# Attention and routed experts on one core: the attention turn in another order, with v's sum and the expert pieces' low halves on VectorE

## The reference

```python
x = L0_attn_x
xn = _layernorm(x, axis=-1)
x = x + attention(xn, Wq, bq, Wk, bk, Wv, bv, Wo, bo, projection) + moe(xn, router_w, w1, w2)
```

## Time and profile before

| | |
|---|---|
| median of 3 runs | 1439.71 us (1437.99 to 1441.45) |
| the profiled execution | 1445.27 us |
| its span, first to last instruction | 1443.7 us |
| mean granted TensorE clock | 0.914 |
| TensorE busy in the span | 1250.0 us, 87% |
| VectorE | 819.6 us, 57% |
| ScalarE | 662.9 us, 46% |
| GpSimd | 763.1 us, 53% |

### The profile page before, as it was taken

The page is one execution under the profiler, slowest core; times in us unless marked ns, Lnnn a source line. Parts: engine busy times, 40 slices in busy tenths (PEclk is TensorE's granted clock), DMA queues, the critical chain, the costliest instruction groups (busy, mean ns, idle before and its releaser), DMA issues.

```text
span 1443.7 us, 38151 instructions
## 1 busy us (share of the span) xinstructions
PE 1250.0 (87%) x14334; PEld 994.5 (69%) x14334; DVE 819.6 (57%) x1910; ACT 662.9 (46%) x1140; POOL 763.1 (53%) x692
## 2 busy tenths in 40 slices
PE   4787777878787887754999999999999999999997
PEld 2555445455555554532878888888888888888886
DVE  6795867777786968682534444344444444344442
ACT  3776657677576766741323233332323333332322
POOL 3445445565455454673355555565555555565553
PEclk9888888888888878966999999999999999999999
DMA  4032333132323323325964444444444444344451
GB/s 156 28 107 89 118 88 119 30 129 76 107 75 89 118 75 118 119 72 171 279 167 73 80 75 73 71 75 78 75 75 76 79 75 78 68 78 74 78 78 15
DMA packets 156139, 133.73 MB, mean 93 GB/s; under 512 B 93825, under 2 KB 144258, under 8 KB 154946
## 3 DMA queue, kind: packets, MB, share of 16 engines
q1 hardware_dynamic: 122338, 95.58, 23.2%
q0 software_dynamic: 33632, 35.71, 15.6%
HBM read 61.83 MB, written 52.61 MB: 79 GB/s over the span
## 4 chain that ended last, share of the span: by engine, by line
PE 63%; DVE 16%; ACT 9%; DMA 5%; issue 4%; POOL 3%; SPq 0%; DVEq 0%; ACTq 0%; POOLq 0%
PE bank L948 26%; PE bank L964 25%; DMA area<-in_x_dram 3%; DVE area L1332 2%; DVE area L1218 2%; ACT area L512 2%; PE bank L825 2%; PE bank L732 2%; PE bank L811 2%; DVE area L1198 2%; PE bank L741 1%; ACT area L514 1%; ACT area L582 1%; ACT area L565 1%; ACT area L577 1%
## 5 line engine op out<-in xcount | busy, mean ns | idle before, releaser
L948 PE MATMUL bank<-area 128*128 128x256 f16 x3408 | 387.7, 274 | 18.7 <-DMA area<-xg 15.7
L964 PE MATMUL bank<-area 128*128 x3408 | 383.5, 273 | 0.0
L948 PEld LDWEIGHTS bank<-area 128*128 x3408 | 335.2, 98 | 60.1 <-issue 19.5
L1474 DVE TENSOR_SCALAR area<-area 128x512 f16<-128x512 f32 x284 | 128.5, 452 | 423.1 <-ACT area L639 414.3
L964 PEld LDWEIGHTS bank<-area 128*128 128x128 f16 x3408 | 333.3, 98 | 38.8
L1142 POOL DMA_INDIRECT out_dram<-area,mt x142 | 228.5, 1609 | 240.2 <-ACT area L649 213.7
L639 ACT ACTIVATE area<-bank 128x512 f32<-128x512 f32 x284 | 169.5, 597 | 190.0 <-PE bank L948 189.0
L649 ACT ACTIVATE area<-bank,mt 128x256 f32<-128x256 f32 x142 | 59.5, 470 | 329.5 <-PE bank L964 329.5
L1476 DVE SCALAR_TENSOR_TENSOR area<-area 128x512 f16<-128x512 f32 x284 | 196.7, 693 | 9.8
L1050 POOL DMA_INDIRECT slot_table<-area x128 | 136.7, 1068 | 121.3 <-DVE dump_f L1311 78.7
L1135 POOL DMA_INDIRECT xg<-xn_split,mt x142 | 143.5, 1010 | 44.7 <-issue 43.0
(11 more groups left out here) (178 smaller groups left out, 1499.1 us busy)
## 6 DMA issues: line engine op xcount, KB each, us to landing
area<-in_w_dram SPq DMA_DIRECT2D x32, 512.0 KB, 6.3
experts_split<-area SPq DMA_DIRECT2D x32, 512.0 KB, 4.3
area<-experts_split SPq DMA_DIRECT2D x8, 2048.0 KB, 8.0
area<-in_x_dram SPq DMA_DIRECT2D x16, 512.0 KB, 5.9
xn_split<-area SPq DMA_DIRECT2D x16, 512.0 KB, 3.0
out_dram<-area SPq DMA_DIRECT2D x32, 256.0 KB, 2.7
xg<-xn_split,mt POOLq DMA_INDIRECT x142, 2.9
area<-xg SPq DMA_TRANSPOSE x142
```

What stands on the lines that cost most here:

```text
L948: mm = nc.tensor.matmul(big[j][:, i2 * TS:(i2 + 1) * TS], we[:, bass.ds(e * EXPERT + (k * 2048 + wl * 1024 + c * P), P)], moe_xT[t % XT][: ...
L964: mm = nc.tensor.matmul(yb[:, a * D:(a + 1) * D], hT[u % 2][:, c, hl, a * P:(a + 1) * P], we[:, bass.ds(e * EXPERT + off, D)], start=(c == ...
L1474: v.tensor_scalar(hT[u % 2][:, 2 * j:2 * j + 2, 0, :], h32[j], H_SCALE, None, ALU.mult).then_inc(mh_step, 1)
```

## The change

- Key features of groups 0 and 1 (`k_features`, `k_relu`) of batch b + 1 are made at the end of turn b, not at the start of turn b + 1.
- Bank 7, the one of the key-value sums, also serves as a fourth small bank, for seven uses in a ring of its own with one place (`SIDE`); the other uses share the three banks as before.
- x has six half-batch buffers, and both halves of b + 2 are loaded at the start of the turn. The normalised x (`xn`) now has both halves and lies in the memory of the squares (`sq`). `grow` and `shift` are double.
- `v_total` is one reduction on VectorE. `w_low` moves from GpSimd to VectorE and takes the unscaled piece with the factor; ScalarE no longer scales the piece in place but in the rounding.
- The order of all five engines changes: both normalised halves before the key-value copy; the count of ranks after the query features; `o_transpose`, `square_sums`, `square_turn` and `o_project` at other places; `v_over_norm` of the second half at the end of the turn before; `tile_table` behind the key-value copy of the last turn; expert stores later.

```diff
-HALVES = 5
+HALVES = 6
...
-BODY = (attn("rank", "vsum", "kvT") + prep("xT0", "xT1") + attn("cn", "ab0", "ab1", "ab2", "ab3") + prep("xT2", "xT3")
-        + attn("ab4", "ab5", "ab6", "ab7") + prep("v0", "v1", "nrm0", "v2", "nrmT0", "v3") + attn("oT0", "oT1", "out0", "out1")
-        + attn("oT2", "oT3") + prep("v4", "v5") + attn("out2", "out3") + prep("v6", "nrm1", "v7", "nrmT1"))
+BODY = (attn("vsum", "kvT") + prep("xT0", "xT1") + attn("rank", "cn", "ab0", "ab1", "ab2", "ab3")
+        + prep("xT2", "xT3") + attn("ab4", "ab5", "ab6", "ab7") + prep("v0", "v1", "nrm0", "v2", "v3", "nrmT0") + attn("oT0", "oT1")
+        + attn("out0", "out1", "oT2", "oT3") + prep("nrm1", "v4", "v5", "nrmT1") + attn("out2", "out3")
+        + prep("v6", "v7"))
...
+SIDE = ("kvT", "cn", "nrm0", "nrmT0", "out0", "nrm1", "nrmT1")
...
+RINGS = {side: [u for u in SEQ if (u[1] in SIDE) == side] for side in (False, True)}
+SLOT = {use: n for ring in RINGS.values() for n, use in enumerate(ring)}
...
-    n = SLOT[(use[0], use[1], b)]
-    return n % SMALL_BANKS, SEQ[n - SMALL_BANKS] if n >= SMALL_BANKS else None
+    side = use[1] in SIDE
+    n, depth = SLOT[(use[0], use[1], b)], 1 if side else SMALL_BANKS
+    return SMALL_BANKS if side else n % SMALL_BANKS, RINGS[side][n - depth] if n >= depth else None
...
-        small = [bank[0], bank[1], bank[6]]
+        small = [bank[0], bank[1], bank[6], bank[7]]
...
-        xn = view([HT, D], F32)
...
+        xn = sq.rearrange("p a b c -> p (a b c)").rearrange("p (h t d) -> p h t d", h=2, t=HT)
...
             if body and x_next:
                 x_load(sp, b + 2, 0)
+                x_load(sp, b + 2, 1)
             if body:
                 xs_store(sp, b + 1, 0)
+                xs_store(sp, b + 1, 1)
             w_store(sp, b, 0)
             w_load(sp, b, 2)
-            if body:
-                xs_store(sp, b + 1, 1)
             w_store(sp, b, 1)
             w_load(sp, b, 3)
-            w_store(sp, b, 2)
-            if body:
-                w_load(sp, b + 1, 0)
             out_store(sp, b, 0)
             out_store(sp, b, 1)
-            if body and x_next:
-                x_load(sp, b + 2, 1)
+            w_store(sp, b, 2)
+            if body:
+                w_load(sp, b + 1, 0)
+            w_store(sp, b, 3)
+            if body:
+                w_load(sp, b + 1, 1)
             out_store(sp, b, 2)
             out_store(sp, b, 3)
-            w_store(sp, b, 3)
-            if body:
-                w_load(sp, b + 1, 1)
...
-            nc.scalar.activation(w_raw[c % 2], w_raw[c % 2], ACT.Copy, scale=R_SCALE).then_inc(w_scaled, 1)
-            hold(act, w_scaled, e * 4 + c + 1)
-            nc.scalar.activation(w_st[c % 2][:, 0, :], w_raw[c % 2], ACT.Copy).then_inc(w_hi, 1)
+            nc.scalar.activation(w_st[c % 2][:, 0, :], w_raw[c % 2], ACT.Copy, scale=R_SCALE).then_inc(w_hi, 1)
...
-            k_relu(act, b, 0)
-            w_high(act, b, 0, first)
-            k_relu(act, b, 1)
+            k_relu(act, b, 2)
+            k_relu(act, b, 3)
+            if body:
+                xn_high(act, b + 1, 0)
             act.wait_ge(gate_in, b + 1)
             nc.scalar.activation(eg, dl, ACT.Exp, scale=1.0 / R_SCALE).then_inc(gate_exp, 1)
-            k_relu(act, b, 2)
-            w_high(act, b, 1, first)
-            k_relu(act, b, 3)
-            if body:
-                xn_high(act, b + 1, 0)
+            q_relu(act, b, 0, 0, 4)
             nc.scalar.copy(cs_b.rearrange("p h d -> p (h d)"), take(act, phase, "attn", "vsum", b)[:, 0:H * (HD + 1)]) \
                 .then_inc(attn_taken, 1)
-            q_relu(act, b, 0)
+            if body:
+                xn_high(act, b + 1, 1)
+            q_relu(act, b, 0, 4, PAIRS)
             if body:
                 xT_copy(act, phase, b + 1, 0)
             nc.scalar.copy(cn_b.rearrange("p h d -> p (h d)"), take(act, phase, "attn", "cn", b)[:, 0:H * (HD + 1)]) \
                 .then_inc(attn_taken, 1)
-            if body:
-                xn_high(act, b + 1, 1)
-            w_high(act, b, 2)
-            if not body:
-                w_high(act, b, 3)
             act.wait_ge(attn_filled, nth("attn", f"ab{HT - 1}", b))
-            q_relu(act, b, 1)
+            q_relu(act, b, 1, 0, PAIRS)
             if body:
                 xT_copy(act, phase, b + 1, 1)
+            w_high(act, b, 0, first)
+            w_high(act, b, 1, first)
...
+            o_hi(act, b, 1)
             oT_copy(act, phase, b, 0)
-            o_hi(act, b, 1)
             if body:
                 resid_rows(act, b + 1, 0)
                 qk_read_half(act, b + 1, 1, 0, 4)
+                w_high(act, b, 2)
+                squares_copy(act, phase, b + 1, 1)
+            oT_copy(act, phase, b, 1)
+            if not body:
+                w_high(act, b, 2)
                 w_high(act, b, 3)
-                resid_rows(act, b + 1, 1)
-            oT_copy(act, phase, b, 1)
-            if body:
-                v_copy(act, phase, b + 1, HT)
-                v_copy(act, phase, b + 1, HT + 1)
-                last_copies(act, phase, b + 1)
+                return
+            v_copy(act, phase, b + 1, HT)
+            v_copy(act, phase, b + 1, HT + 1)
+            w_high(act, b, 3)
+            k_relu(act, b + 1, 0)
+            resid_rows(act, b + 1, 1)
+            v_copy(act, phase, b + 1, HT + 2)
+            v_copy(act, phase, b + 1, HT + 3)
+            k_relu(act, b + 1, 1)
...
+            if tl == 0:
+                wait_read(pe, "prep", f"xT{2 * half + 1}", b)
...
+            if t == 0:
+                wait_read(pe, "prep", "nrmT1", b)
+                if b == 0:
+                    pe.wait_ge(bias_split, 1)
...
-            k_features(pe, b, 0)
             for g in range(1, NT // 2):
-                k_features(pe, b, g)
+                if g > 1:
+                    k_features(pe, b, g)
                 kv_sum(pe, b, 2 * g - 2)
                 kv_sum(pe, b, 2 * g - 1)
-                if g == RANK_AT[phase]:
-                    count_ranks(pe, phase, b)
             kv_sum(pe, b, NT - 2)
-
+            kv_sum(pe, b, NT - 1)
+            q_features(pe, b, 0, 0)
             dst = small_ap(phase, "attn", "vsum", b, pe)
             pe.wait_ge(vsum_ready, b + 1)
             nc.tensor.matmul(dst[:, 0:H * (HD + 1)], cfeat[:, :], vsum.rearrange("p h d -> p (h d)"),
                              start=True, stop=True).then_inc(attn_filled, 1)
-            kv_sum(pe, b, NT - 1)
-            q_features(pe, b, 0, 0)
             dst = small_ap(phase, "attn", "kvT", b, pe)
             pe.wait_ge(kvt_copied, b + 1)
             for m in range(KC):
                 mm = nc.tensor.transpose(dst[:, m * P:(m + 1) * P], kvt[:, m * P:(m + 1) * P], ident32[:, :])
             mm.then_inc(attn_filled, 1)
+            if body:
+                x_transpose(pe, phase, b + 1, 0)
             q_features(pe, b, 0, 1)
-            if body:
-                x_transpose(pe, phase, b + 1, 0)
-
+            count_ranks(pe, phase, b)
...
+            if body:
+                x_transpose(pe, phase, b + 1, 1)
             q_features(pe, b, 1, 1)
-            if body:
-                x_transpose(pe, phase, b + 1, 1)
...
+            if not body:
+                o_transpose(pe, phase, b, 0)
+                o_project(pe, phase, b, 0)
+                o_transpose(pe, phase, b, 1)
+                o_project(pe, phase, b, 1)
+                return
+            qk_project(pe, b + 1, 0, False)
+            v_project(pe, phase, b + 1, 0)
...
+            square_turn(pe, phase, b + 1, 0)
             o_transpose(pe, phase, b, 0)
-            if body:
-                qk_project(pe, b + 1, 1, False)
+            qk_project(pe, b + 1, 1, False)
             o_project(pe, phase, b, 0)
             o_transpose(pe, phase, b, 1)
-            if body:
-                v_and_squares(pe, phase, b + 1, 1, attended=b)
...
+            square_sums(pe, phase, b + 1, 1)
+            v_project(pe, phase, b + 1, HT)
+            v_project(pe, phase, b + 1, HT + 1)
+            square_turn(pe, phase, b + 1, 1)
+            k_features(pe, b + 1, 0)
+            o_project(pe, phase, b, 1)
+            v_project(pe, phase, b + 1, HT + 2)
+            v_project(pe, phase, b + 1, HT + 3)
+            k_features(pe, b + 1, 1)
...
+            if phase == "tail":
                 scatter(pool, b)
-                w_low(pool, b, 2)
-                w_low(pool, b, 3)
                 return
-            x_low(pool, b + 1, 1)
-            w_low(pool, b, 2)
+            for half in range(2):
+                x_low(pool, b + 1, half)
             scatter(pool, b)
-            w_low(pool, b, 3)
             norm_refine(pool, b + 1, 1)
-            v_total(pool, b + 1)
...
+            if b > 1:
+                dve.wait_ge(resid_ready, b * 2 - 2)
...
+        def w_low(dve, e, c):
+
+            dve.wait_ge(w_hi, e * 4 + c + 1)
```

(49 more changed lines are left out.)

125 lines of the change are left out of this document (48 added, 77 removed).

## The result

| | before | after |
|---|---|---|
| median of the runs, us (same chip) | 1440.58 (1437.99 to 1445.14, 4 runs) | 1394.35 (1393.00 to 1398.30, 4 runs) |
| ratio | | 0.968 [0.9648, 0.9712] |
| span of the profiled execution, us | 1443.7 | 1391.0 |

The change makes the kernel 3.2% faster, 46 us. 1378 was forecast, with 1346 to 1415 as the range: the direction and the range held, the gain was forecast a third too large (61 us).

What follows compares the result with a forecast made beforehand. It took the attention turns as bound by a chain in VectorE's order with waits: 67.6 + 6 x 69.5 + 68 + 69 = 621.6 us against 682.8. The 61.2 less, from the 1439.7 median, gave 1378 us, range 1346 to 1415.

Steps and rivals of the forecast that it cites:

- What sets the turn: Attention turns: a chain in VectorE's order with waits for other engines in it; a period was 79.1 us before.
- The walk: One attention turn added up in VectorE's new order from the start of v's sum; a period of 69.5 us.
- The x load: VectorE's wait for the second half of x before the row sums goes away; 5.7 us a turn.
- Rival 3: SP's queue stays blocked before the x loads, so the x wait remains: 34 us more, 1412 us; chance 0.04.
- The reduction: v's sum over eight tiles, moved from GpSimd to VectorE: 2.3 us a turn, upper bound 5.1.
- Rival 4: Strided reduction at 5.9 ns an element, 12 us; at 14 us the program takes 1460 us, slower; chance 0.04.
- The expert pieces: Four low halves a turn moved from GpSimd to VectorE: 4.7 us more there, against 4.7 us of locks removed.
- The locks of 4.7 us a turn: VectorE instructions held until GpSimd's end: 3.3 us at the normalising ones, 1.4 at a small copy; to go away.
- The refinement as the wait that remains: GpSimd's norm refinement at the turn's end, 7.1 us plus 1.5 (0 to 2.4) for locks; VectorE waits for it.
- The seventh period: Last attention period: 68 us, with row sums and factors missing (6 us less) but the output projection and refinement staying.
- Start and end: Start to first key-value copy 67.6 us (69.0 before); last copy to experts 69 us (57.6 before).
- Rivals 1 and 2: Locks vanish, refinement hidden: period 65.5, 1350 us, chance 0.15; TensorE or ScalarE waits return: 74 to 75, 1413, 0.15.

Runs made afterwards that it cites:

- e11: Changed kernel with five x half-buffers, the second half's load back at the end of SyncE's turn; 1426.9 and 1428.8 us in two executions.
- e10: Changed kernel with v's sum reading eight neighbouring numbers instead of numbers 264 words apart (output not the reference's); 1385.74 us, ratio 0.9576 to before.
- e9: e7 with the division of v's second half by the norm ahead of the choice of experts instead of behind it; 1376.36 us, ratio 0.9509 to before.
- e12: Kernel before with only six x halves, the normalised x placed in the squares' memory; 1418.22 us, ratio 0.9815 to before.
- e8: Changed kernel with the expert pieces' four low halves back on GpSimd and ScalarE's extra scaling pass restored; 1431.09 us, ratio 0.9911 to before.
- e6: Changed kernel, division of v's second half by the norm moved behind the next turn's v sum and choice of experts; 1395.91 us, ratio 0.9651 to before.
- e3: Changed kernel with v's sum back on GpSimd as three adds behind the refinement, on a stalling chip; 1454.38 us, ratio 0.983 to before.
- e7: e6 with v also summed over the tiles by three VectorE adds in place of the strided reduction; 1388.77 us, ratio 0.9608 to before.

## Why the prediction was right, and where it was not

**What sets the turn: right, with one part left out.** A chain in VectorE's order with waits for others in it. e11 (a wait put back counts in full), e10 (1.6 us off an instruction moves the six periods by 1.6, all seven by 1.2 on average) and e9 show it. The walk doesn't count the sixteen scatters between the placing and the refinement. By its own numbers they would end near 57 us (35.0, and 21.5 us as in the trace of before), just ahead of the 59.0 that it takes; measured from the start of v's sum at 269.89 they end at 59.8 and the refinement starts at 60.5. That the omission cost nothing in the sum is luck: the two come out at nearly the same time.

**The x load: right, 5.7 us forecast.** 5.5 us in the changed kernel (e11), 4.1 in the kernel before (e12). The 5.7 was read from one turn; the six had 6.7 on average. Rival 3 fell.

**The reduction: the term that was mis-sized.** 2.3 us forecast, 3.87 measured. The upper bound of 5.1 took it in; the value chosen did not. The walk said 69.5; with 1.6 more it says 71.1, and the six periods are 71.15. With the contiguous price in place (e10) the ratio is 0.9576, and times the 1439.7 us of the runs shown that is 1378.7 us, the forecast within 1 us; the interval gives 1375 to 1382, so the last microsecond is luck. Of the 16 us between 1378 and 1394 the stages of the profiled executions hold 8.5: 9.9 in the six periods (the stride's 1.6 each), 2.6 in the seventh, less 2.4, 1.2 and 0.4 at the start, the end and the experts. The other 7 come from which execution was profiled: before's lay 5.6 us above the median that the forecast started from, after's 1.4 below its own. Rival 4 had the right mechanism and a wrong size (5.9 ns an element; 1.9 measured), and its argument against itself was false: L1263 has the stride between rows of 256 neighbours, not between neighbouring reads. The Trainium skill has the rule (SBUF — State Buffer, "Door 1: The DMA port swizzle", the note on cachelines): an access that leaves a 16-byte line pays a penalty, so four neighbouring fp32 are free and a larger step is not. Both durations of the reduction agree with it, and it should have been weighed. The rule that was weighed, no faster mode for tensor_reduce, is not contradicted by the 2.28 us. The forecast's own range of 1358 to 1400 is narrower than its bounds: with the three taken at their ends together it is 1354 to 1418.

**The expert pieces: right, by the mechanism that the step named.** Mean 1.24 us each, 1.17 forecast. The locks of 4.7 us a turn went: the eight normalising instructions take 2.67 us where they took 4.64 + 1.37, the small copy 0.23 where it took 1.74, 4.9 us together; 1.4 came back in the cast. With the pieces on GpSimd again (e8) there are 4.2 us of locks, on other instructions. The step's rule against it, to move work off a saturated engine, would have had the turn grow by 7 us; e8 follows it and loses 35 us. The prediction gave that rule without its second half: the same section of the Trainium skill (Perfetto Trace Analysis, "Optimizing Scalar/DVE Operations") adds that VectorE and GpSimd share a read port, so that moving work between these two might not help, and e8 agrees.

**The refinement as the wait that remains: right.** 8.9 us in the turn shown (8.2 to 8.9 over all) against 8.6 forecast and 7.1 before; VectorE waits 1.7 us for it in the first six turns. The walk didn't say that removing this wait is worth nothing so long as the division itself is late for TensorE (e6).

**The seventh period: wrong by 2.6 us** (70.6 against 68). It has VectorE 55.4 us busy instead of 64, but the refinement can't come earlier, since the scatters stand in front of it. VectorE's part of the norms is done at 542.15 us; on GpSimd the last scatter and the refinement's first instruction are

```profile
543.34 0.96 POOL L1049 DMA_INDIRECT slot_table<-area  x1 [0.30 <-issue]
544.33 0.46 POOL L1037 TENSOR_TENSOR area<-area 128x128 f32<-128x128 f32 x1
```

and the wait for its end grows to

```profile
DVE area L1256 <- POOL area L1042: 5.0, 1, 5.0
```

The step took 6 us off for the missing row sums and factors and put 4.5 back; by this row it is nearly all that has to be put back, and 2.2 us of it are the scatters'. **Start and end** were 2.4 and 1.2 us better than forecast, which cancels it.

**Rivals 1 and 2 fell.** The wait for the refinement didn't vanish, and the six periods are 71.15 us, neither 65.5 nor 74 to 75; the granted clock in them is 0.86, against 0.83 before.

**Not settled.** With e8 and e11 as prices (3.1 to 3.4 and 5.5 us a turn) the two parts make more than the 7.9 us by which the six periods shrank, so the rest (the sum of v on VectorE, the fourth bank, the new order) cost about 1 us a turn, no more than the stride does. This supposes that the parts add up, and that e8 prices the pieces alone. With e12's 4.1 in place of e11's 5.5 the rest comes out as 0.4 to 0.7 us gained, so not even its sign is shown. The fourth bank and the order weren't tried alone. e3, the one run with the sum on GpSimd, ran on the stalling chip.

## What to carry to other kernels

Price an instruction by a row with its own access pattern: step between neighbouring elements, not just the count. When a wait is moved away, ask at once who needs the result that was waited for; e6 gained nothing, and e9, with the same instructions in another order, gained 1.0% on e7. Work is worth moving onto the fullest engine if on the other one it locks the fullest for as long, and stands ahead of a result for which the fullest waits. Lay the other engine's queue beside the walk too: here sixteen short instructions, none of them long, decide as often as VectorE when the refinement can start.
